# Joining attention and feed-forward into one program, with the first feed-forward tile prepared during the last batch steps

## What is computed

```python
def _L0_xattn_ref(q, k, v, Wq, Wk, Wv, Wo, bo, g):
    ...
    qh = jnp.einsum('bcn,oc->bon', q, Wq).reshape(b, HEADS, DIM_HEAD, -1)
    ...
    qh = jax.nn.softmax(qh, axis=-2) * SCALE
    kh = jax.nn.softmax(kh, axis=-1)
    context = jnp.einsum('bhdn,bhen->bhde', kh, vh)
    out = jnp.einsum('bhde,bhdn->bhen', context, qh)
    ...
    norm = jnp.maximum(jnp.sqrt(jnp.sum(out * out, axis=1, keepdims=True)), 1e-12)
    return out / norm * g * np.sqrt(DIM)

def _L0_ffn_ref(x, c1_w, c2_w, w1, w2t):
    ...
    inter = xf @ c1_w.T @ c2_w.T
    n_blocks = INTER // SPARSITY
    blk = inter.reshape(B * T, n_blocks, SPARSITY)
    idx = jnp.argmax(blk, axis=-1) + jnp.arange(0, INTER, SPARSITY)
    w1_g = w1[idx]
    w2_g = w2t[idx]
    h = jax.nn.relu(jnp.einsum('bkm,bm->bk', w1_g, xf))
    out = jnp.einsum('bk,bkm->bm', h, w2_g)
    return out.reshape(B, T, M)
x = x + _L0_xattn_ref(_layernorm(x, axis=-1), ctx_4096, ctx_4096, L0_xattn_Wq, L0_xattn_Wk, L0_xattn_Wv, L0_xattn_Wo, L0_xattn_bo, L0_xattn_g)
x = x + _L0_ffn_ref(_layernorm(x, axis=-1), L0_ffn_c1_w, L0_ffn_c2_w, L0_ffn_w1, L0_ffn_w2t)
```

## Time and profile before

| | us |
|---|---|
| median of 3 runs | 860.18 |
| lowest and highest run | 857.99, 1524.28 |
| the profiled execution's own time | 858.17 |
| its span, first to last instruction | 856.3 |
| last attention instruction ends (ACT, L424) | about 436.6 |
| first `hide` of tile 0 begins | 453.97 |
| `turn_x` to `turn_x` in the middle tiles | 24.8 |
| one middle batch step of attention | 12.8 |

### The profile page before, as it was taken

How to read it: one execution, slowest core, us unless ns; L and a number is a source line. 1 busy time by engine, 2 the same in 40 slices (tenths; PEclk the granted TensorE clock), 3 DMA queues, 4 the chain that set the end, 5 groups by cost and what they waited for, 6 DMA issues and landing times. The chain is left out here.

```text
span 856.3 us, 14103 instructions
## 1 busy us (share of the span) xinstructions
PE 803.4 (94%) x4832; PEld 545.6 (64%) x4832; DVE 647.0 (76%) x954; ACT 409.1 (48%) x819; POOL 445.0 (52%) x520
## 2 busy tenths in 40 slices
PE   4999999999999999999947999999999999999998
PEld 2455555555555555555525878787887878788876
DVE  5788888988888888888745676777766777776674
ACT  3688888888788888888721111111111111111111
POOL 5687786787687787787403333343333334433332
PEclk9999999999999999999978999999999999999999
DMA  6223323323323323321220100111111011111000
GB/s 158 75 64 90 91 61 91 90 62 90 90 62 90 90 61 90 90 62 55 69 62 25 38 27 11 38 38 38 38 38 37 2 38 38 38 38 38 13 4 22
DMA packets 30101, 48.07 MB, mean 56 GB/s; under 512 B 4816, under 2 KB 13136, under 8 KB 30032
## 3 DMA queue, kind: packets, MB, share of 16 engines
q1 hardware_dynamic: 29360, 46.19, 18.4%
q10 hardware_dynamic: 672, 0.98, 0.5%
HBM read 38.77 MB, written 8.39 MB: 55 GB/s over the span
## 5 line engine op out<-in xcount | busy, mean ns | idle before, releaser
L637 POOL TENSOR_TENSOR ranked<-mask,rank 128x256 bf16<-128x256 bf16 (+1 forms) x64 | 66.8, 1044 | 198.8 <-DVE mask L788 198.8
L476 PE MATMUL po<-ET,ctxT 128*64 128x512 f32 x256 | 137.0, 618 | 3.1
L479 PE MATMUL po<-QT,G 128*64 128x512 f32 x256 | 136.8, 617 | 0.0
L256 POOL TENSOR_TENSOR Q<-Q,qrec 128x1024 f32<-128x1024 f32 x64 | 120.5, 1905 | 11.6 <-DVE qrec L344 11.5
L711 ACT ACTIVATE hT_hi<-turned 128x256 fp32r<-128x256 f32 (+1 forms) x64 | 34.9, 545 | 188.5 <-PE turned L920 188.5
L304 DVE TENSOR_REDUCE qmax<-slot 128x16 f32<-128x1024 f32 x64 | 78.1, 1220 | 37.7 <-PE slot L528 37.7
L909 PE MATMUL hidden<-weights_hi,xT_hi 128*128 128x512 f32 (+1 forms) x256 | 97.3, 380 | 1.4 <-DVE xT_lo L770 1.4
L909 PE MATMUL hidden<-weights_lo,xT_hi 128*128 128x512 f32 (+1 forms) x256 | 95.2, 372 | 0.0
L909 PE MATMUL hidden<-weights_hi,xT_lo 128*128 128x512 f32 (+1 forms) x256 | 94.7, 370 | 0.0
L933 PE MATMUL acc<-weights_hi,hT_hi 128*128 128x512 f32 x224 | 92.0, 411 | 0.0
L393 ACT ACTIVATE ET<-turn_e 128x512 f32<-128x512 f32 x128 | 76.7, 599 | 31.5 <-PE turn_e L453 31.5
(11 more groups left out here) (98 smaller groups left out, 1623.4 us busy)
## 6 DMA issues: line engine op xcount, KB each, us to landing
c_in<-in_ctx SPq DMA_DIRECT2D x64, 128.0 KB, 2.8
x_in<-in_x SPq DMA_DIRECT2D x64, 128.0 KB, 2.6
stage<-in_ffn_w SPq DMA_DIRECT2D x32, 225.0 KB, 2.9
attn_out<-po_sb SPq DMA_DIRECT2D x32, 128.0 KB, 2.3
attn<-attn_out SPq DMA_DIRECT2D x16, 256.0 KB, 2.8
xr<-in_x SPq DMA_DIRECT2D x16, 256.0 KB, 3.0
out<-result SPq DMA_DIRECT2D x16, 256.0 KB, 2.0
ctxT<-in_ctxT SPq DMA_DIRECT2D x31, 128.0 KB, 2.0
```

The costliest lines, as they stand in the source:

```text
L256: nc.gpsimd.tensor_tensor(half, half, qrec[1 - par][:, s, :].unsqueeze(2).broadcast_to([P, HALF, D]), ALU.mult).then_inc(q_scaled, 1)
L476: nc.tensor.matmul(po[0:C, :], ctxT[1 - par][:, m, :], ET[m % 2][:], start=(m == 0), stop=(m == NT - 1)).then_inc(p_mm, 1)
L479: nc.tensor.matmul(po[C:P, :], G[par][:, m, :], QT[m % 2][:], start=(m == 0), stop=(m == HT - 1)).then_inc(out_mm, 1)
```

## The change

The two programs become one, `program`, in one block. These are the parts:

1. SBUF: `attn`, `x2`, `mask`, `ranked`, `behind`, `h_sb`, `result`, `xT_hi`, `xT_lo`, `hT_hi`, `hT_lo`, `z_split` and `z_wide` of the feed-forward become views of attention's `E`, `Q`, `c_high`, `c_low`, `wk_hi`, `wk_lo`, `x_high`, `x_low` and `c_in`. PSUM: `inter` and `hidden` are halves of `slot0` and `slot1`, `turned` is `turn_e` and `turn_q`, `acc` is `po` and `pre` is `gp`. `G` has one buffer. `scaled_attn` is gone (in place in `attn`), the residual's x is loaded into `x2` itself, and the squares and the normalized tile share `work`, which is `stage0`; `inv_wide` is `stage1`.
2. The weights, c2 in four parts and the ranks become 37 staged items: two per step up to step 6, then one per step up to step 29. POOL rounds the c2 parts at steps 25 to 28 and DVE subtracts, behind the moments of that step.
3. The preparation of tile 0 is spread over the steps: squares at 29, `norms` and the floor at 30, `widen`, `spread_norms` and `residual` at 31, `normalize`, `turn_x` and `hide` of chunk 0 at 32, the z part, the first two `project` and `hide` of chunk 1 at 33.
4. The inverse norm of every tile: instead of root on ACT, floor and reciprocal on DVE, there is a floor on DVE straight from PSUM, then POOL raises 128 x 8 values to -0.5 (`invert`). `widen` stands on DVE behind the block maximum of chunk 2, and `spread_norms` on PE behind `hide` of chunk 2.
5. SP loads the attention output and the residual's x of a later tile apart: the first once the tile before it in that buffer is scaled, the second after that tile's result was stored.

```diff
+def items(g):
+
+    if g < 7:
+        return [2 * g, 2 * g + 1]
+    return [g + 7] if g + 7 < ITEMS else []
...
+        attn = [sb("attn0", [P, N])[:], E[0][:, 0, :]]
+        x2 = [sb("x20", [P, N])[:], E[0][:, 1, :]]
+        work, inv_wide = stage[0], stage[1][:].rearrange("p (b c) -> p b c", c=C)
...
+        inter, hidden = ([s[:, i, :] for i in range(2)] for s in slot)
+        turned, acc, pre = [turn_e, turn_q], po, gp
...
+                def invert(a):
+                    pool.wait_ge(norm_max, a + 1)
+                    if later(a):
+                        pool.wait_ge(inv_widened, a)
+                    nc.gpsimd.tensor_tensor(inv[:], norm[:], neg_half[:].broadcast_to([P, 2 * NT]),
+                                            ALU.pow).then_inc(norm_inv, 1)
...
+                def split_c2(i):
+
+                    cols = slice((i - WEIGHT_ITEMS) * C2_COLS, (i - WEIGHT_ITEMS + 1) * C2_COLS)
+                    dve.wait_ge(stage_hi, i + 1)
                     for r in (SPARSE, 3 * SPARSE):
                         q = slice(r, r + SPARSE)
-                        nc.vector.tensor_tensor(c2_split[q, :], c2_raw[q, :], c2_split[q, :].bitcast(fp32),
-                                                ALU.subtract).then_inc(ffn_consts_done, 1)
+                        nc.vector.tensor_tensor(c2_split[q, cols], stage[i % 2][q, 0:C2_COLS],
+                                                c2_split[q, cols].bitcast(fp32), ALU.subtract).then_inc(c2_done, 1)
...
+                    if not last:
+                        norm_floor(p + 1)
+                    block_max(p, 2)
+                    if not last:
+                        widen(p + 1)
+                    gate(1)
...
+                    if known == B:
+                        normalize(0, 0)
+                    if known == B - 1:
+                        widen(0)
...
+                    for i in items(g) if known >= 0 else []:
+                        if WEIGHT_ITEMS <= i < WEIGHT_ITEMS + C2_ITEMS:
+                            split_c2(i)
+                    if known == B - 2:
+                        norm_floor(0)
+                    if known == B - 1:
+                        residual(0, 0)
...
+                    if known == B + 1:
+                        project(0, 0, 0)
+                        project(0, 0, 1)
+                        hide(0, 0, 1)
+                    else:
+                        turn(1)
...
+                    if known == B - 2:
+                        norms(0)
+                    if known == B - 1:
+                        spread_norms(0)
                     turn(2)
                     products(1)
+                    if known == B:
+                        turn_x(0, 0)
```

More of the change, by code:

```diff
@@ L75, in attention_phase @@
         po_bias = sb("po_bias", [P, 1])
-        ident = shared["ident"]
-        stage = [sb(f"stage{i}", [P, SPLIT]) for i in range(2)]
+        stage = [sb(f"stage{i}", [P, N]) for i in range(2)]
         x_in = [sb(f"x_in{i}", [P, N]) for i in range(2)]
@@ L141, in attention_phase @@
         heads = lambda ap: ap.rearrange("p a (h d) -> p (a h) d", d=D)
-        FFN_CONSTS = 4
+        NB = CHUNK // SPARSE
+        half = lambda ap, i: ap.bitcast(bf16)[:, i * CHUNK:(i + 1) * CHUNK]
+        attn = [sb("attn0", [P, N])[:], E[0][:, 0, :]]
+        x2 = [sb("x20", [P, N])[:], E[0][:, 1, :]]
+        work, inv_wide = stage[0], stage[1][:].rearrange("p (b c) -> p b c", c=C)
+        mask, ranked, behind = ([half(ap, i) for i in range(2)] for ap in (E[0][:, 2, :], E[0][:, 3, :], E[1][:, 0, :]))
@@ L144, in attention_phase, with tiles @@
+        def tiles(tile):
+            for p in range(TILES):
+                tile(p, p // 2, p % 2, p == TILES - 1)
         with nc.Block() as block:
@@ L196, in _ @@
                 steps(step)
+                outs = out.rearrange("(t b) c n -> t (b c) n", b=2)
+                for p in range(TILES):
+                    par = p % 2
+                    if p < TILES - 2:
+                        sp.wait_ge(scaled, p + 1)
+                        load_attn(p + 2, par)
+                    sp.wait_ge(o_done, p + 1)
+                    sp.dma_start(outs[p], result[par]).then_inc(out_stored[par], 16)
+                    if p < TILES - 2:
+                        load_xr(p + 2, par)
                 for s in stored:
                     sp.wait_ge(s, 16 * (B // 2))
+                for s in out_stored:
+                    sp.wait_ge(s, 16 * (TILES // 2))
             @block.gpsimd
@@ L854, in _ @@
+                steps(step)
                 block_max(0, 0)
@@ L858, in _, with fold_vo @@
             @block.tensor
             def _(pe):
+                def fold_vo():
+                    pe.wait_ge(vo_in, 32)
+                    for h in range(HEADS):
+                        last = nc.tensor.matmul(gp[0:C, h * C:(h + 1) * C], wv[:, h, :], woT[:, h, :],
+                                                start=True, stop=True)
+                    last.then_inc(vo_mm, 1)
                 def norms(a):
                     pe.wait_ge(squared, a + 1)
+                    if a == 0:
+                        pe.wait_ge(consts_in, 32)
+                        pe.wait_ge(g_ready, B - 3)
+                    elif a == 1:
+                        pe.wait_ge(g_ready, B)
@@ L865, in norms @@
                     for t in range(NT):
[L866 removed]
+                        last = nc.tensor.matmul(pre[:, 2 * t:2 * t + 2], work[:, t * P:(t + 1) * P], batch_of[:],
                                                 start=True, stop=True)
```

944 lines of the change are left out of this document (466 added, 478 removed).

## The result

The changed kernel takes 854.73 us (median of 6 runs, 852.52 to 855.85) against 859.61 of the kernel before: ratio 0.9947, interval 0.993 to 0.9965. That is 4.9 us less, where 8.1 were forecast. The direction and the range were right, the size was not. One run of the kernel before took 1524.28 us and is left out of the ratio. A second group of runs gave 0.9964 (0.9949 to 0.9978).

A forecast was written before the change was run, and what follows sets the result against it. PE, or rings through PE, was taken to bound both loops, with one hole between them. Against the profiled 858.17 us, -24.4 + 1.7 + 4.8 + 3.8 + 6.0 = -8.1 gave 850.1 us, range 841 to 862 (about 0.8).

The forecast's parts named there:

- What bounds the kernel: Attention and tile loops: limited by PE (busy 94% of the span) or rings through PE, with one hole between them.
- Handover, -24.4: Last turn_q of attention to first turn_x of the tile loop: 20.7 us instead of 45.1.
- Step 0, +1.7: First batch step: a second slice on POOL ahead of var_eps of batch 1, all 1.7 us of it paid.
- c2, +4.8: Steps 25 to 28: DVE's c2 subtractions delay the sums for POOL's scaling of Q, 1.2 us a step.
- The upper bound's mechanism: Steps 25 to 28: 2.4 us a step if both c2 subtractions also wait for POOL's 0.57 us power.
- Steps 30 to 32, +3.8: End of attention: norms adds 0.8 us, widen and residual ahead of the sums 2.3, turn_x and hide 0.7.
- The tile loop, +6.0: Feed-forward tiles: widen, 0.43 us, moves into the ring behind chunk 2's block maximum, paid in 14 periods.
- A slow power: Tile loop: POOL's power costs per column, 3.2 us, and delays widen; 22 us more, 872 us; chance 0.10.
- the 2.8 us window: Tile loop: time from the second subtraction's end to chunk 2's mask, taken to hide POOL's new power.
- POOL takes the port first: Tile loop: POOL's ranks of chunk 2 start ahead of widen, 1.2 us more a tile, 867 us; chance 0.07.
- Attention pays less: Attention: PE and ACT absorb most of c2 and steps 31 and 32, widen costs 0.3; 842.5 us; chance 0.14.
- The preparation does not overlap: Handover: the drain cannot take the z part and hide without new waits, half of 24.4 goes; 862 us; chance 0.07.

The follow-up runs named there:

- the late split: The changed kernel with DVE's two subtractions per c2 slice moved to the end of their step, behind the reciprocals for POOL's scaling of Q: 851.99 us.

## Why the prediction was right or wrong

The forecast of 8.1 us was 3.2 too large. Against the profile it missed 2.5 us in the c2 term and 1.8 in the handover; the start, the steps around 31, the tile loop and the rest came out 1.8 better than forecast. The remaining 0.7 is that both profiled executions were faster than their medians, the changed kernel's by more (2.2 us against 1.4).

*What bounds the kernel* was right. Both loops have PE at their centre, and most edits moved the time by the wait that they opened or closed on PE; 0.08 us a tile stand in no wait.

*Handover, -24.4: found -22.6.* The step that failed is "I take off 1.2 for waits on ACT's copies, now covered by `hide`". PE did not wait for ACT in the old drain: its 7.0 us are matmuls in a row, so nothing was there to cover. In fact the z part made a new wait of 0.85 us, ahead of the place where `hide` stands. Without the deduction the drain would have been 11.0; it took 11.24. Moving `hide` into the hole gave the 0.9 back. The other 0.3 is between `norms` and `turn_x` (11.24 instead of 10.9). The rows place it: the projections start 1.09 us after `norms` (451.03 to 452.12), where the sum had 0.79 for `norms` alone and nothing for the two transposes between them.

*Step 0, +1.7: found +0.9 in the profile, 2.3 on average.* ACT's wait was 5.25 as forecast (5.4). What followed differed between executions, and the profiled one was the best of eight. With one slice the start is the same to 0.2 us in every profile.

*c2, +4.8: found +7.3 in the profile, 8.0 on average, 7.0 to 7.7 by taking it away.* This is the largest miss, and the second step that failed. Two things were wrong. The first is the size: "a quarter is about 0.55 us each", worked out from a long row at the end of attention, was 0.62 in the step (1.27 for the pair), and the sum of `Q` no longer overlaps the end of the moments, so 1.44 a step instead of 1.2. This lies within the bounds. The second is missing from the sum: a wait of 1.64 us on PE in four steps running, behind which the granted clock fell in up to two of them, 1.6 us each. The prediction put the clock at nothing here; it looked for falls only in the middle, where the profile of before had them. That the wait brings the fall on is likely and not shown. The upper bound's mechanism (both subtractions waiting for the power) did not occur: the power itself took 0.94 instead of 0.57 us.

*Steps 30 to 32, +3.8: found +3.4*, and by the way named: the addition moved to POOL took 1.64 of it away.

*The tile loop, +6.0: found +5.8.* The mechanism was right, the closeness of the size is partly luck. `widen` behind the maximum lengthens the ring by 0.33 us, near the lower bound of 0.3 for a partial overlap and not at its full 0.43; that is 4.7 us over 14 periods. Another 0.08 us a tile, 1.1 us, lies between `turn_x` and `norms`, was not in the forecast, and its cause is open.

*The rivals.* "A slow power": the power took 1.66 us, between the fixed price (0.6) and the price per column (3.2): (1.66 - 0.57) / 7 = 0.16 us for each further column, where the rival had 0.38 and the forecast said below 1 us in all. It is hidden all the same, as the 2.8 us window said. The Trainium skill ("GPSIMD Engine Reference", section 3.1) gives about 2.6 cycles per element for elementwise work and has it from an add. The estimate from that figure was 0.02 us for the seven columns; the trace has 1.09 us, so for the power the figure does not hold, and the measurement decides. "POOL takes the port first" did not occur: DVE's `widen` came first in the tile shown, and POOL's ranks stretched by 0.1 us. "Attention pays less" was wrong in its direction: attention paid more. "The preparation does not overlap" was wrong, too; of the 24.4 only 1.8 were lost.

## What to carry to other kernels

When work moves onto an engine that feeds the bottleneck, first look for an engine with a hole at that place: POOL did the same subtraction in nearly twice the time (2.37 against 1.27 us a pair) and for nothing. A deduction for waits that a transfer of work "covers" needs the waits as rows; where the bottleneck's instructions stand in a row, there is none. And a new wait of PE can be priced twice, once by its length and once by what the granted clock does behind it. The second price is not certain: 28 waits of about 1.64 us in the c2 steps had 10 falls behind them, and the 8 waits of 1.46 us in step 32 had none. Last, a term that comes out to 0.2 us, as the tile loop did, can still be two errors that cancel.

## What the runs showed of the hardware

- PE waits of 1.64 us stood in four steps of a loop in which it is otherwise busy almost throughout. Behind none, one or two of the four the granted clock fell from the upper to the lower level for some 3.5 us, and 1.6 us were lost each time. Waits of 1.46 us in step 32 had no such fall behind them in any of eight executions, nor had waits of up to 1.07 us in the late split; one of 1.2 us in a tile had, and four of six waits of 1.5 us ahead of `gp` of step 2.
- GpSimd's power: 0.57 us for one column of 128 values, 1.65 to 1.68 for eight.
- A subtraction of 32x448 on DVE: 0.62 us alone, 1.02 and 2.22 beside GpSimd's multiplication of 128x1024. The same on GpSimd: 1.14 us.
- A table load on ACT took 1.28 us and cost 1.04 us when it stood in the chain; started early by a root of one column, nothing.
